# Output product of a gated state-space block: four fp32 matmuls a tile, or twelve float32r matmuls of rounded halves

## The chip, the cores and the metric

One Trainium2 chip, one core. The metric is the device time of one execution, in microseconds: the median over several runs. TensorE (PE in the profile) multiplies, VectorE (DVE), ScalarE (ACT) and GpSimd (POOL) work on tiles, SyncE (SP) issues the DMAs.

## The reference

`x` is 8 x 2048 x 256 in fp32. The block is a simplified state-space layer, then a feed-forward layer on weights and inputs rounded to a 4-bit grid in blocks of 16, each followed by a residual sum and a layer norm:

```python
xz = x @ W_in; x_proj, z = split(xz)            # 256 -> 2 * 512
x_conv = silu(causal_conv4(x_proj) + conv_b)
ssm = x_conv @ W_xproj                          # 512 -> 33: delta, B, C
delta = softplus(ssm[..., 0])
h_mean = einsum('bld,bln->bdn', x_conv, delta * B) / L
y = einsum('bdn,bln->bld', h_mean, C) + D * x_conv
y = y * silu(z)
x = layernorm(x + y @ W_out)                    # 512 -> 256, the product of this change
gate, up = fp4(x) @ fp4(w_gate).T, fp4(x) @ fp4(w_up).T
h = silu(gate) * up                             # 704
x = layernorm(x + fp4(h) @ fp4(w_down).T)
```

## The kernel before

The sequence axis is cut into 32 groups (`NSUP`) of 512 positions, four groups a batch element. A step of the kernel is a *unit*: group index `g_` and j = 0 to 3. Each engine has one queue, written out by hand; `walk(body)` runs the same loop over units on each of them, and semaphores couple them. Within a unit the engines work at different things: u = 4 g_ + j is the channel block whose input projection is made; v = u - 1 the block in the convolution; w = u - 20 the block (five groups behind, `LAG`) whose output y is formed and gated; and `to, tx, tg, td, tz` = w - 4 to w - 8 are tiles of 128 positions in the output product and first layer norm, in the rounding of x, in gate and up, in the down product and in the output. Up to `g_ == LAG` there is only input work and weight preparation (the opening), from `g_ > NSUP` on no input work (the end part).

Before the change the gated block is one fp32 buffer `g`, 128 x 2 x 4 x 512, two groups deep. VectorE's `skip` (L1128) writes D * x_conv + y from bank `pc` into it, GpSimd (L460) multiplies it in place by silu(z) and signals `g_ready`; in the end part VectorE does it in one step (`gated`, L1245) after TensorE's `skip_product` (L593). One unit later `output_projection` (L608) multiplies a tile of all four channel blocks with `wout`, in fp32:

```python
for c in range(NB):
    mm = pe.matmul(bank[:, 0:DM], g[:, (second(s) + 1) % 2, c, j * P:(j + 1) * P],
                   wout[:, c, :], start=(c == 0), stop=(c == NB - 1))
```

The other large products are made of float32r halves already, three products for one (`split_product`, L532). TensorE's order in a steady unit: gate and up (bank pgu), input projection (pa), transposes of h (L572), y product (L583), output product (L608), [j = 2: partial state L619], state projection (L635, which writes bank pc and waits for `skip`), transposes (L648, L658), z projection (pb), [j = 3: L678], down product (pd, L532 with wd).

What follows an output product: VectorE sums with the residual (L1218), ScalarE squares (L802), GpSimd makes the norm's factors (L411, L413, L415, on 128x1), ScalarE applies them (L904, `r1_rows`), and in the next unit VectorE rounds the tile to codes (L1001, L1005, L1009, L1013, L1019, L1022, the same lines as for h: 704 wide for h, 256 for x). On GpSimd the order in a steady unit is: norm of `tz`, x products (L427), history (L446), gate (L460), `conv_sum` (L450), norm of `to` (L411 to L415), h products (L470, L472). On ScalarE, in j = 0 units, softplus with two table loads (L808 to L983) comes right behind L904; in the next unit follow the squares (L802), the magnitude of x (L867) and the silu of the gate (L872), for which VectorE's L1190 waits.

Of the kernel before, what the change touches and what calls it, by code (L numbers as in the profile page):

```python
# [52 lines left out]
def block_kernel(nc, x, x_t, W_in, conv_w, conv_b, W_xproj, D_skip, W_out, w_gate, w_up, w_down, out):  # L53
# [26 lines left out]
    with ExitStack() as ctx:  # L80
# [13 lines left out]
        wout = sb("wout", [P, NB, DM])  # L94
# [30 lines left out]
        g = sb("g", [P, 2, NB, ST])  # L125
# [76 lines left out]
        yd_done = sem("yd_done")  # L202
        g_ready = sem("g_ready")
        xres_landed = [sem("xres_landed0"), sem("xres_landed1")]
# [37 lines left out]
        scratch = sb("scratch", [P, 5 * GW + 2 * FF + KM * P])  # L242
        flat_g = g[:, :, :, :].rearrange("p a b c -> p (a b c)")
        raw_g = scratch[:, 0:GW]
        raw_u = flat_g[:, GW + 9 * (GW // QB):2 * GW + 9 * (GW // QB)]
        raw_d = scratch[:, 5 * GW:5 * GW + 2 * FF]
        twice_d = scratch[:, 5 * GW + 2 * FF:5 * GW + 2 * FF + KM * P]
        quant_w = [scratch[:, n * GW:(n + 1) * GW] for n in range(1, 4)]
        w_big = [scratch[:, 4 * GW:5 * GW], flat_g[:, 0:GW], raw_g]

        at = [0]

        def over_scratch(width):

            at[0] += width
            assert at[0] <= scratch.shape[1]
            return scratch[:, at[0] - width:at[0]]

# [8 lines left out]
        GQ = GW // QB  # L267
        w_small = [[flat_g[:, GW + (3 * n + r) * GQ:GW + (3 * n + r + 1) * GQ] for r in range(3)]
                   for n in range(3)]
# [57 lines left out]
        def _(q):  # L327
# [19 lines left out]
            def body(g_, s, b):  # L347
                i = g_ - LAG
                for j in range(TPS):
# [6 lines left out]
                    if exists(w + 1):  # L356

                        n, half = (j + 1) % 2, 16 * (2 * i + (j + 1) // 2 + 1)
                        wait_apart(q, (xc_saved[n], half), (sz_saved[n], half), (g_ready, w))
                        q.dma_start(xl[:, n, :], xc_hbm[w + 1]).then_inc(xl_landed[n], 16)  # L360
                        q.dma_start(zl[:, n, :], sz_hbm[w + 1]).then_inc(zl_landed[n], 16)
# [22 lines left out]
        def _(pool):  # L384
# [33 lines left out]
            def body(g_, s, b):  # L418
                i = g_ - LAG
                for j in range(TPS):  # L420
# [35 lines left out]
                    if p2 and g_ <= NSUP:  # L456

                        pool.wait_ge(yd_done, w + 1)
                        pool.wait_ge(zl_landed[j % 2], 16 * (2 * i + j // 2 + 1))
                        pool.tensor_tensor(g[:, second(s) % 2, j, :], g[:, second(s) % 2, j, :], zl[:, j % 2, :],  # L460
                                           ALU.mult).then_inc(g_ready, 1)
                    if p1 and g_ > LAG:
                        conv_sum()
                    if exists(to) and g_ <= NSUP:
                        layer_norm(to, ssq1_done, r1_ready, rs1_eps, rs1_done, nm1_done, sum1, ssq1, rs1, nm1)
                    if exists(tg):
# [6 lines left out]
                                           spread(qsh[:, :, 1]), ALU.mult).then_inc(hprod_done, 1)  # L473
                    if j == 0 and exists(v):
# [38 lines left out]
        def _(pe):  # L513
# [62 lines left out]
            def y_product(j, s, b, g_, v, w):  # L576

                wait_apart(pe, (h_ready, b - 1 if s == 0 else b), (ct_ready, g_ - LAG + 1), (g_ready if g_ > NSUP else yd_done, w),
# [16 lines left out]
            def output_projection(j, s, i, g_, to, tz):  # L595
# [8 lines left out]
                if i == 1 and j == 0:  # L604
                    pe.wait_ge(w_landed, 32)
# [93 lines left out]
            def body(g_, s, b):  # L699
                i = g_ - LAG  # L700
                tail = exists(g_ - 1, NSUP)
                for j in range(TPS):
# [19 lines left out]
                    if g_ > NSUP:  # L722
# [48 lines left out]
        def _(act):  # L771
# [10 lines left out]
            def weight_magnitudes(u):  # L782

                if u in BIG_AT:
                    n = BIG_AT.index(u)
                    act.wait_ge(wq_link, CODED[n])
                    act.activation(w_big[n][:, 0:W_WIDTH[n]], quant_w[n][:, 0:W_WIDTH[n]], ACT.Abs, scale=TWO22)\
# [29 lines left out]
            def body(g_, s, b):  # L817
                i = g_ - LAG
                tail = exists(g_ - 1, NSUP)
                for j in range(TPS):  # L820
# [47 lines left out]

                    def gate_silu():
# [37 lines left out]
                    if g_ > NSUP:  # L907
# [16 lines left out]
                        if exists(tz):  # L924
                            out_rows()
                        continue
                    if g_ <= LAG:
# [5 lines left out]
                        weight_copies(u)  # L933
                        if exists(v):
                            conv_copy()
                        if j == 2:
# [23 lines left out]
                    if exists(tz):  # L960
                        out_rows()
                    if p1 and td < 0:
# [35 lines left out]
        def _(dve):  # L998
# [87 lines left out]
            def body(g_, s, b):  # L1086
                i = g_ - LAG
                tail = exists(g_ - 1, NSUP)
                for j in range(TPS):
# [32 lines left out]
                    def skip():  # L1122
                        dve.wait_ge(y_pe, w + 1)
                        dve.wait_ge(xl_landed[j % 2], 16 * (2 * i + j // 2 + 1))
                        at_least(dve, o_pe, 4 * i - 4)
                        if w == 0:
                            dve.wait_ge(w_landed, 32)
                        dve.scalar_tensor_tensor(g[:, second(s) % 2, j, :], xl[:, j % 2, :], dsk[:, j:j + 1], pc[:, :],  # L1128
# [110 lines left out]
                    def gated():  # L1239
                        if w == 4 * (NSUP - LAG + 1):  # L1240
                            dve.wait_ge(g_ready, w)
                        dve.wait_ge(y_pe, w + 1)
                        dve.wait_ge(zl_landed[j % 2], 16 * (2 * i + j // 2 + 1))
                        at_least(dve, o_pe, 4 * i - 4)
                        dve.tensor_tensor(g[:, second(s) % 2, j, :], pc[:, :], zl[:, j % 2, :],  # L1245
                                          ALU.mult).then_inc(g_ready, 1)
# [26 lines left out]
                    if g_ <= LAG:  # L1273
# [9 lines left out]
                        weight_codes(u)  # L1283
                        if j == 1 and 2 <= g_ < LAG:
# [80 lines left out]
```

## Time and profile before

| | us |
|---|---|
| median of 3 runs | 1985.98 (1985.72 to 1989.41) |
| the profiled execution, its own time | 1988.75 |
| its span, first to last instruction | 1987.0 |
| TensorE busy | 1920.3 (97%) |
| VectorE busy | 1578.8 (79%) |
| ScalarE busy | 1265.9 (64%) |
| GpSimd busy | 1102.5 (55%) |
| mean granted TensorE clock | 0.986 of 2.4 GHz |

Busy shares are means over an opening, a steady part and an end part. An engine's busy time counts its instructions from issue to end, waits for a memory port included. A record of a matmul is listed with its modelled end, so the distance between starts tells more than its duration.

### The profile page before, as it was taken

How to read it: one execution, taken by the hardware profiler on the slowest of the kernel's cores; microseconds unless marked ns; L12 is line 12 of the kernel's file. 1: busy time of each engine (PE TensorE's matmuls, PEld its weight loads, DVE VectorE, ACT ScalarE, POOL GpSimd, SP SyncE). 2: the span in 40 equal slices, each digit the busy share in tenths (PEclk: the TensorE clock that was granted, in tenths of full speed). 3: DMA queues.
4: the chain of work that ended last, by engine and by line, in shares of the span. 5: the costliest groups of instructions: out<-in, count | busy, mean ns of one | idle time of the engine just before them, and what ended most of it. 6: DMA issues, size and time to landing. Idle time of an engine off the chain costs nothing. (4 is left out here: it accounts for less than half of the span.)

```text
span 1987.0 us, 34279 instructions
## 1 busy us (share of the span) xinstructions
PE 1920.3 (97%) x10180; PEld 1540.1 (78%) x10180; DVE 1578.8 (79%) x3549; ACT 1265.9 (64%) x2617; POOL 1102.5 (55%) x1758
## 2 busy tenths in 40 slices
PE   6898999999999999999999999999999999999996
PEld 5665788888878888888788788888888888777775
DVE  5645788878888888888888888888788887788885
ACT  6776666666666666666666666666666666544443
POOL 3434555556555656655556665565565556555553
PEclk8898999999999999999999999999999999999998
DMA  5234233232322322323223232232323223222210
GB/s 167 96 122 144 91 100 103 89 109 99 102 100 98 99 95 99 109 94 109 96 85 107 99 109 96 99 104 88 109 99 101 100 88 99 69 65 73 72 38 16
DMA packets 120309, 190.60 MB, mean 96 GB/s; under 512 B 15040, under 2 KB 49728, under 8 KB 120128
## 3 DMA queue, kind: packets, MB, share of 16 engines
q1 hardware_dynamic: 120128, 188.42, 28.5%
q8 instruction: 85, 1.39, 0.3%
q14 instruction: 96, 0.79, 0.1%
HBM read 104.48 MB, written 83.89 MB: 95 GB/s over the span
## 5 line engine op out<-in xcount | busy, mean ns | idle before, releaser
L532 PE MATMUL pgu<-wgu_hi,xqT 128*128 128x512 f32 (+1 forms) x1536 | 427.1, 386 | 7.6 <-issue 6.5
L532 PEld LDWEIGHTS pgu<-wgu_hi,xqT 128*128 128x128 f32 x1536 | 278.7, 189 | 72.0 <-issue 9.9
L532 PE MATMUL pd<-wd_hi,hqT 128*128 128x256 f32 (+1 forms) x1536 | 315.9, 297 | 5.2 <-issue 2.1
L532 PEld LDWEIGHTS pd<-wd_hi,hqT 128*128 128x128 f32 (+1 forms) x1536 | 247.7, 190 | 26.6 <-issue 4.8
L1019 DVE SCALAR_TENSOR_TENSOR scratch<-scratch 128x256 f32<-128x256 f32 (+2 forms) x258 | 171.8, 666 | 96.7 <-ACT scratch L898 77.4
L411 POOL TENSOR_SCALAR rs<-ssq 128x1 f32<-128x1 f32 x256 | 72.4, 283 | 310.3 <-issue 297.3
L532 PE MATMUL pgu<-wgu_lo,xqT 128*128 128x512 f32 (+1 forms) x768 | 228.0, 378 | 0.0
L1104 DVE SCALAR_TENSOR_TENSOR acc<-xps,cw,acc 128x512 f32<-128x512 f32 x256 | 200.3, 782 | 30.8 <-POOL acc L450 26.2
L608 PE MATMUL pd<-wout,g 128*128 128x256 f32 x864 | 215.4, 392 | 0.0
L802 ACT ACTIVATE scratch<-scratch,sum 128x256 f32<-128x256 f32 x256 | 130.2, 509 | 123.4 <-DVE scratch L1164 118.4
L472 POOL TENSOR_TENSOR scratch<-hnq,qsh 128x704 f32<-128x704 bf16 x128 | 188.7, 1474 | 0.0
L608 PEld LDWEIGHTS pd<-wout,g 128*128 128x128 f32 x864 | 155.2, 189 | 42.6 <-issue 25.8
L413 POOL TENSOR_TENSOR rs<-rs,nhalf 128x1 f32<-128x1 f32 x256 | 170.4, 666 | 21.6
L532 PE MATMUL pd<-wd_lo,hqT 128*128 128x256 f32 x640 | 181.6, 284 | 0.0
L872 ACT ACTIVATE scratch<-pgu 128x704 f32<-128x704 f32 x128 | 96.6, 755 | 116.5 <-PE pgu L532 116.5
L450 POOL TENSOR_TENSOR acc<-acc,tap 128x512 f32<-128x512 f32 x128 | 164.3, 1284 | 11.4 <-ACT tap L846 11.4
L635 PEld LDWEIGHTS pc<-wxp,xcs 128*128 128x128 f32 x1024 | 134.6, 194 | 38.5 <-ACT xcs L829 21.6
L460 POOL TENSOR_TENSOR g<-g,early 128x512 f32<-128x512 f32 x112 | 143.1, 1278 | 35.5 <-DVE g L1128 35.2
L532 PEld LDWEIGHTS pgu<-wgu_lo,xqT 128*128 128x128 f32 x768 | 143.2, 189 | 23.5
L415 POOL TENSOR_SCALAR nm<-sum,rs 128x1 f32<-128x1 f32 x256 | 131.4, 513 | 43.8 <-POOL rs L413 43.8
L635 PE MATMUL pc<-wxp,xcs 128*128 128x33 f32 x1024 | 128.7, 271 | 24.6 <-ACT xcs L829 17.5
L427 POOL TENSOR_TENSOR scratch<-xnq,qsx 128x256 f32<-128x256 bf16 x128 | 81.3, 635 | 118.6 <-DVE xnq L1022 115.5
(140 smaller groups left out, 4489.8 us busy)
## 6 DMA issues: line engine op xcount, KB each, us to landing
sz_hbm<-szs SPq DMA_DIRECT2D x128, 256.0 KB, 2.0
xc_hbm<-xcs SPq DMA_DIRECT2D x128, 256.0 KB, 2.0
early<-xc_hbm SPq DMA_DIRECT2D x128, 256.0 KB, 2.7
early<-sz_hbm SPq DMA_DIRECT2D x128, 256.0 KB, 3.0
xin<-in_x_t_dram SPq DMA_DIRECT2D x32, 512.0 KB, 4.7
xres<-in_L_attn_x_dram SPq DMA_DIRECT2D x128, 128.0 KB, 2.4
out_dram<-scratch SPq DMA_DIRECT2D x128, 128.0 KB, 1.7
early<-in_L_attn_W_in_dram SPq DMA_DIRECT2D x2, 512.0 KB, 4.7
```

Of the source, the lines that this page charges most:

```text
L413: pool.tensor_tensor(rs[:, :], rs[:, :], nhalf[:, :], ALU.pow).then_inc(rs_done, 1)
L415: pool.tensor_scalar(nm[:, :], total[:, :], rs[:, :], -1.0 / DM, ALU.mult, ALU.mult)\
L450: pool.tensor_tensor(acc[:, j % 2, :], acc[:, j % 2, :], tap0[:, j % 2, :], ALU.add).then_inc(tap_done, 1)
L460: pool.tensor_tensor(g[:, second(s) % 2, j, :], g[:, second(s) % 2, j, :], zl[:, j % 2, :], ALU.mult).then_inc(g_ready, 1)
L472: pool.tensor_tensor(blocks(hq[:, 0:FF]), blocks(hnq[:, :]), spread(qsh[:, :, 1]), ALU.mult).then_inc(hprod_done, 1)
L532: mm = pe.matmul(bank, lhsT, rhs, start=(m == 0), stop=(m == len(pairs) - 1))
L608: mm = pe.matmul(bank[:, 0:DM], g[:, (second(s) + 1) % 2, c, j * P:(j + 1) * P], wout[:, c, :], start=(c == 0), stop=(c == NB - 1))
L635: mm = pe.matmul(pc[:, t * NX:(t + 1) * NX], xcs[:, jb % 2, t * P:(t + 1) * P], wxp[:, jb, :], start=True, stop=True)
L802: act.activation(dev[:, 0 if ssq is ssq1 else 1, :], r, ACT.Square, bias=total[:, :], scale=-1.0 * DM, accum_out=ssq[:, :]).then_inc(ssq_d ...
L872: act.activation(hbuf[:, 0:FF], pgu[:, 0:FF], ACT.Silu).then_inc(sg_ready, 1)
L1019: return dve.scalar_tensor_tensor(v, big, HALF_STEP, v, ALU.max, ALU.add)
L1104: dve.scalar_tensor_tensor(acc[:, jb % 2, :], xps[:, jb % 2, k:k + ST], cw[:, jb, k:k + 1], acc[:, jb % 2, :], ALU.mult, ALU.add).then_inc ...
```

## The change

The gated block is kept as two float32r halves, `g_hi` (rounded) and `g_lo` (the rest), and so is W_out (`wo_hi`, `wo_lo`). The output product of a tile is hi x hi, hi x lo and lo x hi: twelve float32r matmuls in place of four fp32 ones. Both halves are kept for one group only: blocks and tiles swap places in the buffer from group to group, so that a block may be written once the tile that lay there is multiplied. `skip` and the gate now work in a small buffer `gx` (two blocks); ScalarE copies it to `g_hi` (`gate_high`), GpSimd subtracts (`gate_rest`) and signals `g_ready`. The signal after the gate alone is `gate_done`. In ScalarE's queue `gate_high` stands, in the opening, behind `conv_copy` and ahead of `split_input`, `c_copy` and softplus; in the steady part behind `out_rows` (L887); in the end part last in the unit. W_out is split once in the opening (units 17 and 18). The weights are quantised in place, with buffers rearranged. In the end part `skip_product` goes ahead of the output product. The core of the diff:

```diff
-        g = sb("g", [P, 2, NB, ST])
+        g_hi = sb("g_hi", [P, NB, TPS, P], F32R)
+        g_lo = sb("g_lo", [P, NB, TPS, P], F32R)
...
+        def gated_block(half, i, c):
+            return half[:, c, :, :] if i % 2 == 0 else half[:, :, c, :]
+
+        def gated_tile(half, i, c, t):
+            return half[:, c, t, :] if i % 2 == 0 else half[:, t, c, :]
...
@@ gpsimd
-                        pool.tensor_tensor(g[:, second(s) % 2, j, :], g[:, second(s) % 2, j, :], zl[:, j % 2, :],
-                                           ALU.mult).then_inc(g_ready, 1)
+                        pool.tensor_tensor(gx[:, j % 2, :], gx[:, j % 2, :], zl[:, j % 2, :],
+                                           ALU.mult).then_inc(gate_done, 1)
+
+                    def gate_rest():
+                        pool.wait_ge(g_high, w + 1)
+                        pool.tensor_tensor(gated_block(g_lo, i, j), tiles_of(gx[:, j % 2, :]),
+                                           gated_block(g_hi, i, j), ALU.subtract).then_inc(g_ready, 1)
                     if p1 and g_ > LAG:
                         conv_sum()
+                    if p2 and g_ <= NSUP:
+                        gate_rest()
...
                         pool.tensor_tensor(blocks(hq[:, 0:FF]), blocks(hnq[:, :]),
                                            spread(qsh[:, :, 1]), ALU.mult).then_inc(hprod_done, 1)
+                    if p2 and g_ > NSUP:
+                        gate_rest()
...
@@ tensor, output_projection
+                pairs = []
                 for c in range(NB):
-                    mm = pe.matmul(bank[:, 0:DM], g[:, (second(s) + 1) % 2, c, j * P:(j + 1) * P],
-                                   wout[:, c, :], start=(c == 0), stop=(c == NB - 1))
-                mm.then_inc(o_pe, 1)
+                    high, low = gated_tile(g_hi, i - 1, c, j), gated_tile(g_lo, i - 1, c, j)
+                    pairs += [(high, wo_hi[:, c, :]), (high, wo_lo[:, c, :]), (low, wo_hi[:, c, :])]
+                split_product(bank[:, 0:DM], DM, pairs).then_inc(o_pe, 1)
...
@@ tensor, end part
+                        if p2:
+                            skip_product(j, i, w)
                         if exists(to):
                             output_projection(j, s, i, g_, to, tz)
-                        if p2:
-                            skip_product(j, i, w)
...
@@ scalar
+                    def gate_high():
+                        act.wait_ge(gate_done, w + 1)
+                        at_least(act, o_pe, 4 * (i - 1) + j + 1)
+                        act.activation(gated_block(g_hi, i, j), tiles_of(gx[:, j % 2, :]), ACT.Copy).then_inc(g_high, 1)
...
+                        if u == 17:
+                            act.wait_ge(w_landed, 32)
+                            act.activation(wo_hi[:, :, :], wout, ACT.Copy).then_inc(wo_h, 1)
...
@@ vector
-                        at_least(dve, o_pe, 4 * i - 4)
+                        at_least(dve, g_ready, w - 1)
...
+                        if u == 18:
+                            dve.wait_ge(wo_h, 1)
+                            dve.tensor_tensor(wo_lo[:, :, :], wout, wo_hi[:, :, :], ALU.subtract).then_inc(wo_l, 1)
```

## Rows read from the trace of the kernel before

**Rows 1.** Busy time by stretch: steady part, end part. Columns as in the head row.

```profile
400.00:600.00 200.00, 200.00 (x1085) 162.94 (x1085) 164.66 (x379) 134.48 (x281) 119.64 (x191) 1.00 0.31 103
1750.00:1850.00 100.00, 97.54 (x509) 77.97 (x508) 88.98 (x220) 49.69 (x115) 52.33 (x83) 1.00 0.26 80
```

**Rows 2.** Groups of instructions by line: busy, mean ns | idle before, releasers.

```profile
L780 ACT ACTIVATE xt_hi<-xin 128x512 fp32r<-128x512 f32 x64 | 36.6, 623 | 0.2 <-DMA xin<-in_x_t_dram 0.2
```

**Rows 3.** Timeline, steady part: start, us, engine, instruction, [idle before <-releaser].

```profile
1052.33 1.28 POOL L450 TENSOR_TENSOR acc<-acc,tap 128x512 f32<-128x512 f32 x1
...
1053.53 0.89 DVE L1013 SCALAR_TENSOR_TENSOR scratch<-scratch,qsh 128x704 f32<-128x704 f32 x1
...
1054.88 0.28 PE L532 MATMUL pd<-wd_hi,hqT 128*128 128x256 f32 x1
...
1054.98 0.19 POOL L411 TENSOR_SCALAR rs<-ssq 128x1 f32<-128x1 f32 x1 [1.37 <-issue]
...
1055.26 0.55 POOL L413 TENSOR_TENSOR rs<-rs,nhalf 128x1 f32<-128x1 f32 x1
...
1055.54 0.89 DVE L1019 SCALAR_TENSOR_TENSOR scratch<-scratch 128x704 f32<-128x704 f32 x1 [0.59 <-ACT scratch L898]
...
1056.54 0.89 DVE L1022 SCALAR_TENSOR_TENSOR hnq<-scratch 128x704 bf16<-128x704 f32 x1
1056.56 0.71 PE L532 MATMUL pd<-wd_hi,hqT 128*128 128x256 f32 x3
1056.60 0.60 ACT L904 ACTIVATE scratch<-scratch,nm,rs 128x256 f32<-128x256 f32 x1 [0.60 <-POOL nm L415]
...
1059.39 1.53 DVE L1104 SCALAR_TENSOR_TENSOR acc<-xps,cw,acc 128x512 f32<-128x512 f32 x2
...
1062.34 0.88 DVE L1190 TENSOR_TENSOR scratch<-scratch,pgu 128x704 f32<-128x704 f32 x1
...
1063.74 1.99 PE L608 MATMUL pd<-wout,g 128*128 128x256 f32 x8
1063.85 0.75 DVE L1128 SCALAR_TENSOR_TENSOR g<-early,dsk,pc 128x512 f32<-128x512 f32 x1 [0.62 <-PE pc L583]
...
1065.57 0.64 PE L635 MATMUL pc<-wxp,xcs 128*128 128x33 f32 x5
...
1079.24 1.06 PE L619 MATMUL pc<-xct,dB 128*48 128x512 f32 x2
```

**Rows 4.** Timeline of the end part, VectorE and GpSimd.

```profile
1788.85 0.89 DVE L1013 SCALAR_TENSOR_TENSOR scratch<-scratch,qsh 128x704 f32<-128x704 f32 x1
...
1789.01 0.79 POOL L411 TENSOR_SCALAR rs<-ssq 128x1 f32<-128x1 f32 x1 [0.79 <-issue]
...
1790.60 0.97 POOL L415 TENSOR_SCALAR nm<-sum,rs 128x1 f32<-128x1 f32 x1 [0.17 <-POOL rs L413]
1790.60 0.92 DVE L1019 SCALAR_TENSOR_TENSOR scratch<-scratch 128x704 f32<-128x704 f32 x1 [0.52 <-ACT scratch L898]
...
1792.43 0.68 DVE L1245 TENSOR_TENSOR g<-pc,early 128x512 f32<-128x512 f32 x1
...
1792.85 1.43 POOL L472 TENSOR_TENSOR scratch<-hnq,qsh 128x704 f32<-128x704 bf16 x1
...
1794.48 0.42 DVE L1013 SCALAR_TENSOR_TENSOR scratch<-scratch,qsx 128x256 f32<-128x256 f32 x1
...
1795.10 0.89 DVE L1190 TENSOR_TENSOR scratch<-scratch,pgu 128x704 f32<-128x704 f32 x1 [0.20 <-ACT scratch L872]
...
1799.48 0.89 DVE L1013 SCALAR_TENSOR_TENSOR scratch<-scratch,qsh 128x704 f32<-128x704 f32 x1
```

**Rows 5.** Timeline of the opening, first gated block.

```profile
149.38 1.28 ACT L808 ACT_TABLE_LOAD   x1
149.50 1.29 POOL L460 TENSOR_TENSOR g<-g,early 128x512 f32<-128x512 f32 x1
...
149.57 2.58 DVE L1104 SCALAR_TENSOR_TENSOR acc<-xps,cw,acc 128x512 f32<-128x512 f32 x2 [1.90 <-POOL acc L450]
```

More of the change, by code:

```diff
@@ L202, in block_kernel @@
         yd_done = sem("yd_done")
+        gate_done = sem("gate_done")
+        g_high = sem("g_high")
         g_ready = sem("g_ready")
+        wo_h = sem("wo_h")
+        wo_l = sem("wo_l")
         xres_landed = [sem("xres_landed0"), sem("xres_landed1")]
@@ L241, in block_kernel, with from_scratch @@
         zl = early[:, 2 * ST:4 * ST].rearrange("p (n c) -> p n c", n=2)
[L242 to L249, printed above, removed]
+        scratch = sb("scratch", [P, 4 * GW + 9 * (GW // QB) + 2 * FF + KM * P + NB * DM])
         at = [0]
-        def over_scratch(width):
+        def from_scratch(width):
             at[0] += width
@@ L257, in over_scratch, with tiles_of @@
             return scratch[:, at[0] - width:at[0]]
+        raw_g, raw_u, raw_d = from_scratch(GW), from_scratch(GW), from_scratch(2 * FF)
+        quant_w = [raw_g, raw_u, raw_d]
+        twice_d = from_scratch(KM * P)
+        BIG = at[0]
+        w_big = [from_scratch(GW), from_scratch(GW)]
+        w_big.append(w_big[0])
+        GQ = GW // QB
+        w_small = [[from_scratch(GQ) for r in range(3)] for n in range(3)]
+        wout = from_scratch(NB * DM).rearrange("p (c d) -> p c d", c=NB)
+        def tiles_of(ap):
+            return ap.rearrange("p (t n) -> p t n", t=TPS)
+        def gated_block(half, i, c):
+            return half[:, c, :, :] if i % 2 == 0 else half[:, :, c, :]
+        def gated_tile(half, i, c, t):
+            return half[:, c, t, :] if i % 2 == 0 else half[:, t, c, :]
+        later = [0]
+        def over_scratch(width):
+            later[0] += width
+            assert later[0] <= scratch.shape[1]
+            return scratch[:, later[0] - width:later[0]]
         hbuf = over_scratch(2 * FF)
@@ L266, in block_kernel @@
         outb = over_scratch(2 * DM).rearrange("p (t d) -> p t d", t=2)
[L267 to L269 removed]
+        gx = over_scratch(2 * ST).rearrange("p (n c) -> p n c", n=2)
         raw_w, W_WIDTH = (raw_g, raw_u, raw_d), (GW, GW, 2 * FF)
@@ L358, in body @@
                         n, half = (j + 1) % 2, 16 * (2 * i + (j + 1) // 2 + 1)
-                        wait_apart(q, (xc_saved[n], half), (sz_saved[n], half), (g_ready, w))
+                        wait_apart(q, (xc_saved[n], half), (sz_saved[n], half), (gate_done, w))
                         q.dma_start(xl[:, n, :], xc_hbm[w + 1]).then_inc(xl_landed[n], 16)
@@ L576, in y_product @@
             def y_product(j, s, b, g_, v, w):
-                wait_apart(pe, (h_ready, b - 1 if s == 0 else b), (ct_ready, g_ - LAG + 1), (g_ready if g_ > NSUP else yd_done, w),
+                wait_apart(pe, (h_ready, b - 1 if s == 0 else b), (ct_ready, g_ - LAG + 1), (gate_done if g_ > NSUP else yd_done, w),
                            (ssm_added, capped(v, NT)))
@@ L925, in body @@
                             out_rows()
+                        if exists(w) and g_ <= NSUP + LAG - 1:
+                            gate_high()
                         continue
@@ L961, in body @@
                         out_rows()
+                    if exists(w):
+                        gate_high()
                     if p1 and td < 0:
```

19 lines of the change are left out of this document (12 added, 7 removed).

## The prediction

> **What bounds the kernel now.** I read the stretches of time first, then one full round of the periodic part in order of time, then the waits inside it. In the middle of the run TensorE is busy all 200 of 200 us at clock 1.00, VectorE 164.66, ScalarE 134.48, GpSimd 119.64 [rows 1]. There every microsecond taken from TensorE's queue is worth one, as long as nobody else is late. After about 1740 us the picture is another: VectorE 88.98 of 100 and TensorE 97.54 [rows 1], units repeating every 10.63 us (L1013 at 1788.85 and 1799.48 [rows 4]), in a loop through VectorE that does not contain the output product: TensorE's gate/up product, ScalarE's silu, VectorE from L1190 to L1228, TensorE again.
>
> **The output product.** The four matmuls of a tile are eight records (x8), so an fp32 matmul of 256 columns is two. They start at 1063.74 and the next product, L635, at 1065.57 [rows 3]: 1.83 us a tile, 0.229 a record. The new product is twelve float32r matmuls of 256 columns. The down product is made of just these: from the start of its first at 1054.88 to the one at 1056.56 lie 14 of them [rows 3], 0.120 each. Twelve take 1.44. Saved: 0.39 us a tile. What stands ahead of it in the queue, the y product of 48 rows, is the same in either kernel, so I leave that gap as it is.
>
> The Trainium skill (TensorE: Matmul & The Clock Gate, Back-to-back issue gap) gives N/2.4 + 2.5 ns for a warm matmul: 109 ns for 256 columns and twice 107 plus 2.5 for an fp32 record, which would save 0.42 a tile. The rows are 0.120 and 0.229, and the rows decide.
>
> Were TensorE alone in the world, the 108 tiles of the groups up to `g_ == NSUP` (27 groups, `g_` 6 to 32) would give 42 us. The other 20 lie beside the loop above: their sum stands behind VectorE's work on the h block, so they give nothing.
>
> **What is added.** Per tile a ScalarE copy of 128x512 to float32r, 0.62 us by its nearest row [rows 2], and a GpSimd subtraction of 128x512 with two SBUF inputs, 1.28 us by the row of the same shape, L450 [rows 3]. By busy time both fit: a unit is some 14 us (L635 to L619 is 13.67), so 200 us hold 14, and GpSimd goes from 119.64 to about 138, ScalarE from 134.48 to 143. In the steady part the copy stands behind `out_rows`, where ScalarE idles for the transposes; nothing behind it is late. The subtraction stands behind `conv_sum` (L450), directly in front of the layer norm L411, L413, L415. It is this one that I follow, because GpSimd and VectorE hold each other up whenever both read two SBUF operands. Three places show it. L411 on one column took 0.79 when it started at 1789.01, inside VectorE's L1013 (1788.85 to 1789.74), and ended 0.06 after it [rows 4]; free, it takes 0.19 [rows 3]. L415, started together with L1019 at 1790.60, took 0.97. The other way round, two L1104 took 2.58 and not 1.53 [rows 3] when they started at 149.57, 0.07 after GpSimd's L460 had begun [rows 5]: 1.05 lost where 1.22 of L460 was left. So who is late loses what is left of the other, less 0.13 to 0.17. The Trainium skill (SBUF — State Buffer, Who interferes with whom) says that a VectorE instruction with two SBUF inputs contends with a GpSimd one that reads SBUF and that the first to issue keeps the port for its whole length. The trace agrees, with the three numbers above.
>
> *Steady part, hand-over from a j=0 to a j=1 unit [rows 3].* L1013 is issued at 1053.53, L450 ends at 1053.61, and GpSimd, with the next instruction waiting in its queue, issues it a little before that end, by my estimate at 1053.56. VectorE is 0.03 ahead, so I let it win. The subtraction waits to 1054.42 and ends 1.15 later, 1055.57. L1019, issued at 1055.54, goes next, to 1056.46. L411, before at 1054.98, now ends at 1056.52. L1022 follows L1019 by 0.11 and again is just ahead of L413, which ends at 1057.88 (0.42 behind L1022); L415 follows by 0.17 and takes some 0.25, an estimate from L411, the same kind, with 0.19. ScalarE's L904 waits for it: about 1058.35 and not 1056.60, 1.75 late. In a j=1 unit softplus with its two table loads stands right behind L904, so all of ScalarE is 1.75 late, its silu L872 too, and with it VectorE's L1190, which waits for that: 1064.09 and not 1062.34. It takes 0.88, L1128 another 0.75 less an overlap of 0.04: it ends at 1065.68. The state product L635 shares bank pc and waits for L1128: it starts at 1065.73. Before it was 1065.57, and TensorE alone, with two output products shortened (j=0 and j=1), would be there at 1064.79. The wait eats 0.94: this leg is 0.16 slower than before instead of 0.78 faster. From L635 to the partial state L619 at 1079.24 nothing binds anew (VectorE gets there 0.1 to 0.2 before TensorE), so it gains its 0.39: -0.23 so far. In the j=2 unit 3.6 us of L619 let everybody catch up, L411 isn't due until after the subtraction, and the leg to the next j=0 gains 0.39 again. Sum: -0.62 a group of four units where -1.56 was on offer. 108 tiles are 27 groups; 25 of them have this form: -15.5. The first, in which the feed-forward work only begins, gives 4 x 0.39 = -1.6. The last, with TensorE waiting already, 0.
>
> *End part, 16 units with a gate [rows 4].* There L472 ends at 1794.28 and the subtraction is next in line; the gated block was ready at 1793.11 (L1245) and its copy by 1793.8. It starts at 1794.23, 0.25 before L1013 of the x codes (1794.48), and runs to 1795.51. VectorE loses 1.03 - 0.17 = 0.86, of which L1190's wait for ScalarE (it starts 1795.10, could at 1794.82) hides 0.28. L1190 is in the loop: +0.58 a unit, 16 units: +9.3.
>
> *Opening.* At the first gated block ScalarE would go on to softplus at 149.38; `gate_high` now stands in front and waits for L460, which ends at 150.79 [rows 5], and takes 0.62: +2.05. Two later blocks of that group hold the input split and the C copy for about 0.5 each: +1.0. Splitting W_out (128x1024) costs ScalarE about 1.2 (twice L780) and VectorE about 1.3 (L1013's 0.89 for 704 elements, scaled), once, in gaps like the 1.90 that VectorE idled before L1104 [rows 5]; uncovered it would be 2.5. The new load order, the quantisation in place and the waits on `gate_done` at the point where `g_ready` was cost nothing: the same event, at the same place in the DMA queue. In the end part the skip product moves ahead of the output product; a matmul of 128x512 in fp32 is two records, so the output sum finds its operand some 0.9 us later, less the 0.39 saved. I take that as hidden behind VectorE's earlier work; bare, it would be 0.5 x 16 = 8 us, inside the range.
>
> Sum: -15.5 - 1.6 + 9.3 + 3.0 = -4.8 on the profiled execution's 1988.75 (span 1987.0 and 1.75 around it), 1983.95. The median of the runs is 1985.98; the same difference gives **1981.2 us**.
>
> **Rivals.**
> A. The forecast: steady gain mostly eaten in the j=0 to j=1 leg, end part slower. 0.42. Its own range: 1974 to 1989, for the leg's wait may be 0.3 more or less and the opening 1 to 5 us.
> B. At L450's end the subtraction gets the port and not L1013 (they are 0.03 apart). Then VectorE is 1.15 later in every unit but GpSimd's layer norm only 0.5 late; in the j=1 unit L1128 is back in time, and a wait of some 0.25 at L619 is left: -1.3 a group, -33 - 1.6 + 12.3 = -22, 1964. For it: L460 beat L1104 with 0.07 of a lead. Against: L1019 won a tie. 0.22.
> C. The subtraction meets nobody, as L460 and L450 meet only PSUM readers today: -42 + 3 = -39, 1947. The overlaps in rows 3 and 4 speak against it. 0.08.
> D. Slower: the same late layer norm also holds TensorE at the state product in j=0 and j=3 units. There L1128 ends 0.97 before L635 is due, 0.58 once the product is shorter; if VectorE comes more than 0.97 late relative to now in one more unit of each group, the steady gain is gone. From -0.62 it goes to 0 and a little above: 0 to +4, +12.3, so about +14, 2000. For it: three of the four hand-overs have the same order of GpSimd. Against: only j=1 has softplus behind L904. 0.28.
>
> The product by the page's gap instead of the row would only move A by about 1 us and changes no chance.
>
> **How the numbers follow.** A difference of 0.2% is 4 us, about what can be told from none. A lies at -4.8, half of it beyond: faster 0.22, same 0.15, slower 0.05. B and C are faster, 0.30. D is slower 0.25, same 0.03. Together faster 0.52, same 0.18, slower 0.30. The range leaves out C and the far half of D and of the low side of B: 1959 to 2000.
>
> **What would show it.** After: L608 gone, a product of twelve records about 1.44 long before L635; L411 behind L1019 in j=0, 1 and 3 units and L904 later by 1.7; TensorE idle for about 0.9 at L635 in one unit in four; groups of four units 0.6 shorter; in the end part 11.2 and not 10.63 between units, with the x codes' L1013 taking 1.3. A group shorter by 1.3 makes B right, by 1.5 C, one as long as now D. If the end part stays at 10.6, the port is not held by the subtraction, and the forecast is wrong by its largest positive term.

## The result, and the profile of the changed kernel

The changed kernel takes 1997.56 us (median of five runs, 1996.58 to 1998.87), the kernel before 1986.58 beside it on the same chip. The ratio is 1.0051, 95% interval 1.0037 to 1.0066: slower by half a per cent. The forecast was 1981.2, faster by 0.24%. The range held the time, the sign was wrong. The profiled execution took 1996.68 us (span 1994.6), 7.9 more than the profiled one of before (1988.75). The medians lie 11.0 apart: of the five runs of the kernel before, three lie at 1985.7 to 1986.6 and two at 1989.4 to 1989.8, and its profiled execution is near the upper ones.

Busy time by stretch, changed kernel, against [rows 1]. Behind the stretch and its length stand the busy times of TensorE's matmuls, its weight loads, VectorE, ScalarE and GpSimd (with the number of instructions), the granted clock of TensorE, the busy share of the DMA engines and GB/s:

```profile
400.00:600.00 200.00, 198.43 (x1146) 162.99 (x1144) 165.06 (x376) 141.56 (x295) 147.82 (x206) 1.00 0.30 102
1750.00:1850.00 100.00, 91.87 (x518) 73.30 (x518) 91.20 (x204) 52.69 (x116) 60.43 (x91) 1.00 0.23 71
```

In the steady part TensorE now idles 1.57 of 200 us. GpSimd is 28 us busier and not the 18 that fourteen subtractions of 1.28 make. In the end part TensorE has lost 5.7 of 100. The groups say where GpSimd's time is:

```profile
L490 POOL TENSOR_TENSOR g_lo<-scratch,g_hi 128x512 fp32r<-128x512 f32 x128 | 236.3, 1846 | 7.0 <-ACT g_hi L910 7.0
L947 ACT ACTIVATE scratch<-scratch,nm,rs 128x256 f32<-128x256 f32 x128 | 76.8, 600 | 203.8 <-POOL nm L440 203.8
L671 PE MATMUL pc<-wxp,xcs 128*128 128x33 f32 x1024 | 132.1, 274 | 39.6 <-ACT xcs L867 19.5 <-issue 16.8 <-DVE hacc L1186 3.1
```

L490 is the new subtraction: 1.85 us each, though it takes 1.27 when it meets nobody. L947 is the old L904, L440 the old L415: ScalarE waits 203.8 us for the layer norm.

To place the 7.6 us of span, I take the start of the gate/up product of every tile from the timelines; tiles 0 and 4 close the opening and the first group, 4 to 100 are 24 steady groups, 100 to 106 the seam, 106 to 124 the end part with its 16 gated units.

| Stretch | before | changed | difference | forecast |
|---|---|---|---|---|
| start to tile 0 | 190.80 | 196.21 | +5.4 | +3.0 |
| tiles 0 to 4 | 61.73 | 60.61 | -1.1 | -1.6 |
| tiles 4 to 100 | 1402.72 | 1396.58 | -6.1 | -14.9 |
| tiles 100 to 106 | 81.65 | 81.85 | +0.2 | -0.6 |
| tiles 106 to 124 | 191.52 | 201.29 | +9.8 | +9.3 |
| tile 124 to the end | 58.58 | 58.06 | -0.5 | 0 |

The two stretches ahead of tile 4 vary from run to run: with the end part's edit below, the same kernel up to there, tile 0 starts at 195.63 and tiles 0 to 4 take 61.82, so the -1.1 says little.

A steady group was 17.29 + 14.00 + 13.58 + 13.58 us (units j = 2, 3, 0, 1) and is 16.97 + 13.70 + 13.27 + 14.25. Three units are 0.3 shorter, the fourth 0.67 longer. This fourth unit, in order of time (answers to [rows 3]):

```profile
1053.87 0.89 DVE L1065 SCALAR_TENSOR_TENSOR scratch<-scratch,qsh 128x704 f32<-128x704 f32 x1
1053.91 2.00 POOL L490 TENSOR_TENSOR g_lo<-scratch,g_hi 128x512 fp32r<-128x512 f32 x1
1055.61 1.05 DVE L1071 SCALAR_TENSOR_TENSOR scratch<-scratch 128x704 f32<-128x704 f32 x1 [0.32 <-ACT scratch L941]
1056.00 0.71 POOL L436 TENSOR_SCALAR rs<-ssq 128x1 f32<-128x1 f32 x1
1056.77 0.89 DVE L1074 SCALAR_TENSOR_TENSOR hnq<-scratch 128x704 bf16<-128x704 f32 x1
1056.79 1.27 POOL L438 TENSOR_TENSOR rs<-rs,nhalf 128x1 f32<-128x1 f32 x1
1058.23 0.27 POOL L440 TENSOR_SCALAR nm<-sum,rs 128x1 f32<-128x1 f32 x1 [0.17 <-POOL rs L438]
1058.54 0.60 ACT L947 ACTIVATE scratch<-scratch,nm,rs 128x256 f32<-128x256 f32 x1 [2.47 <-POOL nm L440]
1059.16 1.28 ACT L846 ACT_TABLE_LOAD   x1
...
1063.35 0.74 ACT L915 ACTIVATE scratch<-pgu 128x704 f32<-128x704 f32 x1
...
1064.28 0.88 DVE L1242 TENSOR_TENSOR scratch<-scratch,pgu 128x704 f32<-128x704 f32 x1
...
1065.08 0.74 DVE L1180 SCALAR_TENSOR_TENSOR scratch<-early,dsk,pc 128x512 f32<-128x512 f32 x1
1065.15 0.28 PE L567 MATMUL pd<-wo_hi,g_lo 128*128 128x256 f32 x1
1065.92 0.27 PE L671 MATMUL pc<-wxp,xcs 128*128 128x33 f32 x1 [0.49 <-issue]
...
1066.53 0.68 DVE L1251 TENSOR_TENSOR hqT<-pe_,hqT 128x512 fp32r<-128x512 f32 x1
...
1067.13 0.41 DVE L1254 TENSOR_TENSOR hqT<-pb,hqT 128x256 fp32r<-128x256 f32 x1
...
1067.36 0.41 PE L694 MATMUL pe_<-ident,scratch 128*128 128x128 f32 x2
...
1067.69 0.70 PE L567 MATMUL pb<-xt_hi,win_hi 128*128 128x512 f32 x2
```

L1065, L1071, L1074 are the old L1013, L1019, L1022. The subtraction starts 0.04 behind VectorE's division and waits for it (2.00 and not 1.28); the one-column L436 waits for L1071, L438 for L1074. L947 comes 1.32 us behind the gate/up product of its unit (1057.22) where L904 came 0.60 ahead of it. Softplus, the silu L915, L1242 and L1180 follow, and the state product L671 waits for L1180. TensorE's last output matmul starts at 1065.15, the next product at 1065.92 and not 0.12 later: 0.65 of waiting. The profile names no releaser for it ("issue"); the kernel's wait is for L1180, which ends 0.10 before.

Two more waits follow in the same unit. The transposes of x (L694, the old L658) wait for L1251, which ends at 1067.21, the z product for L1254, which ends at 1067.54; each starts 0.15 behind. In the kernel before, the same three starts lie 0.81, 0.47 and 0.14 apart from L635 on (L648, L658, pb), here 0.89, 0.55 and 0.33, in every steady group: another 0.33 in all.

### The profile page after: what moved, and what is told of

The parts are those of the page before. It is cut to its first block and busy times, and to the rows that moved or that the text cites. A ratio compares the mean times of both kernels' runs of the same rounds, so it can differ in the third digit from the quotient of the medians.

```text
span 1994.6 us, 35686 instructions
## 1 busy us (share of the span) xinstructions
PE 1899.6 (95%) x10692; PEld 1536.4 (77%) x10692; DVE 1603.1 (80%) x3550; ACT 1335.0 (67%) x2746; POOL 1348.3 (68%) x1886
## 5 line engine op out<-in xcount | busy, mean ns | idle before, releaser
L1071 DVE SCALAR_TENSOR_TENSOR scratch<-scratch 128x704 f32<-128x704 f32 (+2 forms) x259 | 184.9, 714 | 91.0 <-ACT scratch L941 57.8
L490 POOL TENSOR_TENSOR g_lo<-scratch,g_hi 128x512 fp32r<-128x512 f32 x128 | 236.3, 1846 | 7.0 <-ACT g_hi L910 7.0
L438 POOL TENSOR_TENSOR rs<-rs,nhalf 128x1 f32<-128x1 f32 x256 | 213.8, 835 | 21.3
L436 POOL TENSOR_SCALAR rs<-ssq 128x1 f32<-128x1 f32 x256 | 102.2, 399 | 185.6 <-issue 166.5
L947 ACT ACTIVATE scratch<-scratch,nm,rs 128x256 f32<-128x256 f32 x128 | 76.8, 600 | 203.8 <-POOL nm L440 203.8
L505 POOL TENSOR_TENSOR scratch<-hnq,qsh 128x704 f32<-128x704 bf16 x128 | 182.9, 1429 | 0.0
L475 POOL TENSOR_TENSOR acc<-acc,tap 128x512 f32<-128x512 f32 x128 | 165.2, 1291 | 11.4 <-ACT tap L884 11.4
L671 PEld LDWEIGHTS pc<-wxp,xcs 128*128 128x128 f32 x1024 | 130.1, 196 | 54.0 <-issue 28.0
L671 PE MATMUL pc<-wxp,xcs 128*128 128x33 f32 x1024 | 132.1, 274 | 39.6 <-ACT xcs L867 19.5
L485 POOL TENSOR_TENSOR scratch<-scratch,early 128x512 f32<-128x512 f32 x112 | 143.9, 1285 | 23.5 <-DVE scratch L1180 23.3
L567 PE MATMUL pd<-wo_hi,g_hi 128*128 128x256 f32 x432 | 131.6, 305 | 0.0
L471 POOL COPY hist<-xps 128x3 f32<-128x3 f32 x128 | 27.2, 213 | 153.1 <-ACT acc L878 153.1
```

What stands on the lines that cost most here:

```text
L436: pool.tensor_scalar(rs[:, :], ssq[:, :], 1.0 / DM ** 3, EPS, ALU.mult, ALU.add).then_inc(eps_done, 1)
L438: pool.tensor_tensor(rs[:, :], rs[:, :], nhalf[:, :], ALU.pow).then_inc(rs_done, 1)
L475: pool.tensor_tensor(acc[:, j % 2, :], acc[:, j % 2, :], tap0[:, j % 2, :], ALU.add).then_inc(tap_done, 1)
L485: pool.tensor_tensor(gx[:, j % 2, :], gx[:, j % 2, :], zl[:, j % 2, :], ALU.mult).then_inc(gate_done, 1)
L490: pool.tensor_tensor(gated_block(g_lo, i, j), tiles_of(gx[:, j % 2, :]), gated_block(g_hi, i, j), ALU.subtract).then_inc(g_ready, 1)
L505: pool.tensor_tensor(blocks(hq[:, 0:FF]), blocks(hnq[:, :]), spread(qsh[:, :, 1]), ALU.mult).then_inc(hprod_done, 1)
```

## The experiments

The edits below are made in the changed kernel. [rows 3] and [rows 4] have the same places of before; line numbers of each fence are those of its own kernel. The diffs are shortened. Group and unit lengths are from the starts of the gate/up products.

**No low half.** No subtraction; ScalarE's copy makes the block ready, and the passes that read the low half read the high half.

```diff
-pool.tensor_tensor(gated_block(g_lo, i, j), tiles_of(gx[:, j % 2, :]),
-                   gated_block(g_hi, i, j), ALU.subtract).then_inc(g_ready, 1)
-act.activation(gated_block(g_hi, i, j), ...).then_inc(g_high, 1)
+act.activation(gated_block(g_hi, i, j), ...).then_inc(g_ready, 1)
-high, low = gated_tile(g_hi, i - 1, c, j), gated_tile(g_lo, i - 1, c, j)
+high, low = gated_tile(g_hi, i - 1, c, j), gated_tile(g_hi, i - 1, c, j)
```

> The low half of the gated block is left out: no subtraction on GpSimd, ScalarE's copy alone makes a block ready, and the third kind of pass reads the high half in its place, so the product keeps its twelve passes. All else is the changed kernel. Theory (the subtraction's place on GpSimd makes the layer norm's small operations late in the steady part and holds the x codes' division in the end part): the unit after j = 0's step falls from 14.25 to 13.27 us, the group of four units from 58.19 to 57.2, the end part's unit from 11.23 to 10.6; 25 groups x 1.0 and 16 units x 0.6 are 35 us, so about 1962 us. Rival (the copies on ScalarE or the product's own 1.52 us eat the gain): groups stay at 58.2, end units at 11.2, and the time at 1995 or so.

1960.84 us, ratio to the kernel before 0.9864 (0.9851 to 0.9878). Group 57.22, its fourth unit 13.27, the end part's unit 10.64, first gate/up product at 193.46. The 37 us between this and the changed kernel are what the subtraction costs; the copies on ScalarE stayed, and cost nothing outside the opening: all four steady units are 0.3 shorter than in the kernel before, the end part's unit is as it was.

**A memset in its place.**

```diff
-g_lo = sb("g_lo", [P, NB, TPS, P], F32R)
+g_lo = sb("g_lo", [P, NB, TPS, P])
...
-pool.tensor_tensor(gated_block(g_lo, i, j), ..., ALU.subtract).then_inc(g_ready, 1)
+at_least(pool, g_ready, w)
+pool.memset(g_lo[:, 0:3, :, :], 0.0).then_inc(g_ready, 1)
...
-high, low = gated_tile(g_hi, i - 1, c, j), gated_tile(g_lo, i - 1, c, j)
+high, low = gated_tile(g_hi, i - 1, c, j), gated_tile(g_hi, i - 1, c, j)
```

> The subtraction is replaced by a memset of 1536 columns on GpSimd at the same place behind the same wait (about 1.3 us, writes SBUF and reads nothing); the third kind of pass reads the high half. It leaves out the low half of the gated block. Theory (GpSimd's reads of two SBUF operands and VectorE's hold each other up): the memset takes its 1.3 us always, the x codes' division in the end part is back at 0.43 us, the end part's unit at 10.6, and the steady group near 57.3, since the layer norm's small operations start only 0.3 us late; about 1965 us. Rival (it is the time that GpSimd's queue is taken, not what the operation reads): the steady group stays near 58.2 and the time near 1985 or more.

1964.16 us, 0.9883 (0.9869 to 0.9896). Group 57.34, end unit 10.64. The same hand-over, then the end part, of the memset's timeline:

```profile
1043.12 0.88 DVE L1065 SCALAR_TENSOR_TENSOR scratch<-scratch,qsh 128x704 f32<-128x704 f32 x1
1043.13 1.38 POOL L491 MEMSET g_lo<- 128x1536 f32 x1
1044.61 0.19 POOL L436 TENSOR_SCALAR rs<-ssq 128x1 f32<-128x1 f32 x1
1044.86 0.89 DVE L1071 SCALAR_TENSOR_TENSOR scratch<-scratch 128x704 f32<-128x704 f32 x1 [0.32 <-ACT scratch L941]
1044.88 1.28 POOL L438 TENSOR_TENSOR rs<-rs,nhalf 128x1 f32<-128x1 f32 x1
...
1836.55 1.38 POOL L491 MEMSET g_lo<- 128x1536 f32 x1
1836.82 0.42 DVE L1065 SCALAR_TENSOR_TENSOR scratch<-scratch,qsx 128x256 f32<-128x256 f32 x1
```

GpSimd's queue is taken for longer than by a free subtraction (1.38, all 128 of them between 1.37 and 1.41), beside the same VectorE work, and nobody is held: the division keeps its 0.42. Occupancy of the queue is thus not the cost. It leaves 0.12 a group: it made L436 later, so L438 lost its turn to L1071 by 0.02 and took 1.28. Of the three waits of the fourth unit the last alone is left, at the z product (0.28 behind L694 and not 0.14).

**A copy in its place.**

```diff
-pool.tensor_tensor(gated_block(g_lo, i, j), ..., ALU.subtract).then_inc(g_ready, 1)
+pool.tensor_copy(gated_block(g_lo, i, j), tiles_of(gx[:, j % 2, :])).then_inc(g_ready, 1)
```

> The subtraction is replaced by a GpSimd copy of the same block to the low half: one SBUF operand read and not two, same place, same wait (it leaves out the subtraction, so the low half holds the whole block). Its time alone is between 0.6 and 1.3 us, bounded from the 64-column casts (0.24 us) and the 512-column sums (1.28 us) of GpSimd. Theory (only an operation that reads two SBUF operands holds VectorE's and is held by them): as with the memset, division 0.43 us, end units 10.6, steady group at most 57.4, about 1963 us. Rival (any read by GpSimd does it): division above 0.8 us, end units above 10.8, steady group above 57.6.

1960.51 us, 0.9857 (0.9841 to 0.9874); group 57.22, end unit 10.64. The times are those of my theory, its reason is not:

```profile
1039.28 0.88 DVE L1064 SCALAR_TENSOR_TENSOR scratch<-scratch,qsh 128x704 f32<-128x704 f32 x1
1039.29 1.35 POOL L490 CAST g_lo<-scratch 128x512 fp32r<-128x512 f32 x1
...
1841.96 0.61 POOL L490 CAST g_lo<-scratch 128x512 fp32r<-128x512 f32 x1
1842.22 0.63 DVE L1064 SCALAR_TENSOR_TENSOR scratch<-scratch,qsx 128x256 f32<-128x256 f32 x1
```

Alone the copy takes 0.61. Behind L1064 it takes 1.35, and in the end part it holds L1064 for 0.21. One operand read from SBUF on GpSimd is enough to wait and to be waited for. The copy is cheap because it is short: held, it ends at 1040.64, about where a free subtraction would. So my "only two operands" is refuted for GpSimd's side, and the rival's mechanism holds without its price. The one-operand L411 of [rows 4], held to 0.79, had said so already.

**Layer norm ahead of the subtraction, steady part.**

```diff
-if p2 and g_ <= NSUP:
-    gate_rest()
 if exists(to) and g_ <= NSUP:
     layer_norm(to, ssq1_done, r1_ready, rs1_eps, rs1_done, nm1_done, sum1, ssq1, rs1, nm1)
+if p2 and g_ <= NSUP:
+    gate_rest()
```

> In the steady part alone GpSimd does the layer norm's three small operations ahead of the subtraction and not behind it; the same work. Theory: the scaling of the rows by ScalarE comes back from 1058.54 to about 1056.6, the unit of 14.25 us falls to 13.3, the group from 58.19 to 57.2, the end part stays at 11.23; 25 us less, about 1972 us, faster than the kernel before. Rival (the subtraction then runs against the codes' last step and makes the products of the codes late, so TensorE waits at the transposes instead): the group stays within 0.3 of 58.2 and the time within 5 of 1997.

1989.69 us, 1.0011 (1.0002 to 1.0020): a third of what was expected. The fourth unit was back at 13.27 as forecast, but the second went from 13.70 to 14.15, and in some groups the third too (24 groups: 57.91 on average). In the second unit, j = 3:

```profile
1080.47 1.29 POOL L490 TENSOR_TENSOR g_lo<-scratch,g_hi 128x512 fp32r<-128x512 f32 x1
1080.48 2.03 DVE L1074 SCALAR_TENSOR_TENSOR hnq<-scratch 128x704 bf16<-128x704 f32 x1
1082.59 0.30 POOL L503 TENSOR_TENSOR scratch<-hnq,qsh 128x64 f32<-128x64 bf16 x1 [0.83 <-DVE hnq L1074]
1082.84 1.87 POOL L505 TENSOR_TENSOR scratch<-hnq,qsh 128x704 f32<-128x704 bf16 x1
```

The subtraction now wins by 0.01 and holds L1074 (2.03 for 0.89); the products of the codes behind it on GpSimd end 2.0 us after the unit's gate/up product starts (1082.69) where they ended 0.4 after it. Theory and rival each had half.

**Only in step j = 0.**

```diff
+if p2 and g_ <= NSUP and j != 0:
+    gate_rest()
 if exists(to) and g_ <= NSUP:
     layer_norm(...)
+if p2 and g_ <= NSUP and j == 0:
+    gate_rest()
```

> As norm_first, but only in the step j = 0, whose softplus stands behind the layer norm's rows; in steps 1 to 3 the subtraction stays ahead of the layer norm. The same work. Theory (each place of the subtraction collides with what VectorE does there; only in j = 0 is the layer norm on the path): the unit that took 14.25 us takes 13.3, the one that the last experiment lengthened to 14.15 is back at 13.70, the group is 57.2 us: 24 us less than the changed kernel, about 1974. Rival (the collision is handed on from step to step whatever the order): a group of 57.7 or more, 1985 or more.

1972.20 us, 0.9917 (0.9903 to 0.9931). Group 57.22 (16.98, 13.71, 13.27, 13.27), the very length without a low half. The collision is still there, on an operation that can wait:

```profile
1043.04 0.65 POOL L440 TENSOR_SCALAR nm<-sum,rs 128x1 f32<-128x1 f32 x1 [0.17 <-POOL rs L438]
1043.65 1.27 POOL L490 TENSOR_TENSOR g_lo<-scratch,g_hi 128x512 fp32r<-128x512 f32 x1
1043.66 2.01 DVE L1076 SCALAR_TENSOR_TENSOR hnq<-scratch 128x704 bf16<-128x704 f32 x1
1043.72 0.60 ACT L949 ACTIVATE scratch<-scratch,nm,rs 128x256 f32<-128x256 f32 x1 [0.60 <-POOL nm L440]
```

**End part: the subtraction one unit later.** For j = 0 to 2, behind the product of the x codes.

```diff
 if exists(tx) and g_ > NSUP:
     x_values()
+if g_ > NSUP and p2 and j > 0:
+    gate_rest(w - 1, i, j - 1)
...
-if p2 and g_ > NSUP:
+if p2 and g_ > NSUP and j == 3:
     gate_rest()
```

> In the end part alone the subtraction of units j = 0 to 2 stands one unit later on GpSimd, behind the product of the x codes; that of j = 3 stays. Theory: the x codes' division takes 0.43 us and not 1.3 in 12 of 16 units, which fall from 11.23 to about 10.65 us: 7 us less, 1990 us. Rival (the subtraction holds the codes of the hidden block at its new place, or the copy on ScalarE is what makes the end part longer): units stay at 11.2.

1990.41 us, 1.0014 (1.0004 to 1.0023). Twelve units take 10.64, four 11.21; tiles 106 to 124 take 194.09 and not 201.29. The division beside the subtraction, changed kernel:

```profile
1840.12 1.27 POOL L490 TENSOR_TENSOR g_lo<-scratch,g_hi 128x512 fp32r<-128x512 f32 x1
1840.36 1.31 DVE L1065 SCALAR_TENSOR_TENSOR scratch<-scratch,qsx 128x256 f32<-128x256 f32 x1
1841.60 0.87 DVE L1242 TENSOR_TENSOR scratch<-scratch,pgu 128x704 f32<-128x704 f32 x1
```

and deferred:

```profile
1859.59 0.42 DVE L1067 SCALAR_TENSOR_TENSOR scratch<-scratch,qsx 128x256 f32<-128x256 f32 x1
1860.25 0.89 DVE L1244 TENSOR_TENSOR scratch<-scratch,pgu 128x704 f32<-128x704 f32 x1 [0.23 <-ACT scratch L917]
...
1862.61 1.30 POOL L457 TENSOR_TENSOR g_lo<-scratch,g_hi 128x512 fp32r<-128x512 f32 x1
...
1862.78 0.88 DVE L1055 TENSOR_REDUCE qsh<-scratch 128x44 f32<-128x704 f32 x1
```

At its new place it meets L1055, which has one SBUF input, and neither is longer.

**Both moves.**

> Both moves of the subtraction together: behind the layer norm in j = 0 of the steady part, one unit later in units 0 to 2 of the end part. The same work. Theory (the two costs lie in different stages and add up): 24 + 7 = 31 us less than the changed kernel, about 1966 us, ratio to the kernel before 0.99. Rival (one move gives back part of the other's gain, as at the seam between the stages): 1975 or more.

1964.40 us, 0.9875 (0.9861 to 0.9889). Tiles 4 to 100 take 1373.28, 106 to 124 take 194.11: the two costs add up. This is the best version that computes everything, 1.25% faster than the kernel before.

**And ScalarE's copy last in the opening.** On top of both moves, for `g_ <= LAG`:

```diff
 if exists(v):
     conv_copy()
-if exists(w):
-    gate_high()
 ...
     softplus(g_)
 ...
+if exists(w):
+    gate_high()
 weight_magnitudes(u)
```

> As j0_and_end, and in the opening ScalarE does its copy of the gated block behind the input's split, the C copy and the softplus, and not ahead of them. The same work. Theory (the copy ahead of the softplus and of the split of the next input makes the opening longer): the first gate product comes 1 to 3 us earlier than with j0_and_end, about 1964 us. Rival (in the opening it is the subtraction on GpSimd or the lower granted clock, not the copy's place): the first gate product within 0.7 us of that of j0_and_end, or later.

1966.03 us, 0.9885 (0.9871 to 0.9899), not apart from both moves. The first part went as expected: softplus loads its table at 149.53 and not 151.37, the fourth y product of the group starts at 170.18 and not 172.08. Then TensorE's granted clock falls where it did not before, and tile 0 comes at 199.59, later than with both moves alone (196.71). With both moves alone TensorE has 5.5 us at the lower clock between 156 and 162 us and none from 162 to 189, as in the changed kernel. This kernel:

```profile
156.00:162.00 6.00, 5.29 (x21) 3.59 (x20) 3.70 (x5) 3.85 (x8) 4.54 (x5) 0.81 0.40 129
162.00:170.00 8.00, 6.05 (x22) 2.58 (x21) 5.65 (x6) 6.17 (x11) 5.21 (x6) 1.00 0.53 184
170.00:180.00 10.00, 9.10 (x31) 6.50 (x31) 2.49 (x5) 3.73 (x8) 3.92 (x4) 0.60 0.54 169
180.00:189.00 9.00, 8.31 (x36) 7.09 (x36) 1.47 (x4) 3.62 (x7) 3.40 (x5) 0.69 0.24 75
```

and the changed kernel:

```profile
156.00:162.00 6.00, 6.00 (x20) 4.48 (x20) 4.54 (x5) 3.24 (x6) 4.01 (x5) 0.53 0.40 129
162.00:170.00 8.00, 7.77 (x32) 3.86 (x30) 5.33 (x7) 5.67 (x10) 4.77 (x5) 1.00 0.45 163
170.00:180.00 10.00, 6.71 (x38) 5.12 (x38) 5.14 (x8) 5.91 (x10) 4.90 (x7) 1.00 0.54 162
180.00:189.00 9.00, 8.31 (x50) 6.63 (x48) 2.86 (x10) 5.84 (x13) 5.70 (x11) 1.00 0.46 164
```

0.60 over 10 us and 0.69 over 9 us are 8.0 and 5.6 us at the lower of the two levels (1.2 GHz), where the changed kernel has none; from 156 to 162 us it has 5.6 and this one 2.3. That is some 10 us more at half speed. TensorE had idled 1.95 of the 8 us ahead of the fall, 0.23 in the changed kernel. That this is what made the clock fall is not shown: the changed kernel idles 3.29 of its next 10 us and keeps 1.00 in the 9 behind them. Nor is the clock shown to be all of the 2.9 us.

**No low half in the opening alone.**

```diff
-if p2 and g_ <= NSUP:
+if p2 and LAG < g_ <= NSUP:
     gate_rest()
...
```

(with the copy making these four blocks ready, and their tiles reading the high half twice)

> The low half is left out in the opening alone (four units; the four output tiles that read it take the high half twice): no subtraction there. All else is the changed kernel. Theory (the run without any low half had its first gate product 2.75 us earlier, and that was the subtraction in the opening): first gate product at 193.5 and not 196.2, the steady and the end part unchanged, 2.7 us less: about 1995. Rival (those 2.75 us are the lower granted clock falling on other work, not the subtraction's wait): the first gate product within 1 us of 196.2, with a different length at half clock.

1995.91 us, 1.0036 (1.0023 to 1.0049); the runs overlap with those of the changed kernel (1993.71 to 1997.26, 1996.58 to 1998.87). Tile 0 is at 193.96, 2.25 earlier (expected 2.7). But 0.65 of this was there before the first gated block, where the two kernels do the same: the first y product starts at 142.70 and not 143.35. From that start to tile 0 it is 51.26 us, where the changed kernel and the runs with the layer norm first, only in j = 0, the deferred end part and both moves have 52.86 to 53.05. So the opening's subtractions cost 1.6 to 1.8 us up to tile 0. By tile 4 the difference is lost in what two runs of the same kernel differ by: from the first y product it is 112.7 here, 113.5 in the changed kernel, 114.8 with the end part deferred.

**Sixteen passes.** The halves, copies and subtractions stay, the product is four f32 matmuls of the high halves; the low halves' part is left out.

```diff
-split_product(bank[:, 0:DM], DM, pairs).then_inc(o_pe, 1)
+for c in range(NB):
+    mm = pe.matmul(bank[:, 0:DM], gated_tile(g_hi, i - 1, c, j).bitcast(F32),
+                   wo_hi[:, c, :].bitcast(F32), start=(c == 0), stop=(c == NB - 1))
+mm.then_inc(o_pe, 1)
```

> The halves, their copies, waits and subtractions all stay as in the changed kernel, but the product is four f32 matmuls of the high halves (16 passes), as the kernel before did it. It leaves out the low halves' part of the product. Theory (the product saves 0.31 us a tile wherever TensorE is the bound): units of the steady part grow by 0.3 each but for the one of 14.25 us, in which TensorE waits 0.65 us and can hide it: group 59.1, 25 x 0.93 = 23 us, the end part's unit unchanged at 11.23 (it is not TensorE that bounds it): about 2021 us. Rival (the product isn't on the path, and the gain seen in the units comes from elsewhere): within 5 of 1997.

2017.02 us, 1.0144 (1.0130 to 1.0158). The group is 17.28 + 14.00 + 13.58 + 14.05, 58.92: three units are 0.31 longer, the fourth is 0.2 shorter than with twelve passes. The end part's unit stays at 11.23. So the passes are worth 0.31 us in three of four steady units; the fourth gives 0.2 of it back, since TensorE, being earlier, waits longer at the state product (0.65 us against 0.13); in the end part they are worth nothing. The expectation had the fourth unit unchanged, hence 59.1 and 2021.

## Why the prediction was wrong

**The product.** It saves 0.31 us a tile, not 0.39. Its twelve starts lie 0.118 apart but for the first step, 0.22, behind the y product of 48 rows; together 1.52 from the first to the next product's start, not 1.44. The fp32 product has the same in it: its first step is 0.32, the others 0.216,

```profile
1065.14 0.59 PE L608 MATMUL pd<-wout,g 128*128 128x256 f32 x2
```

the last two of the eight records, 0.43 us ahead of L635 at 1065.57. So the 0.229 of the prediction is no spacing but the product's length over eight, with the long first step in it, while I multiplied the bare spacing of the down product by twelve. The gap that I left "as it is" is the same 0.10 in either kernel, and I counted it in one alone. What makes it was not isolated.

**The fourth unit (hand-over from j = 0 to j = 1).** The links up to L671 were right: tie at L1065, L436 behind L1071, L438 behind L1074, ScalarE, L1242, L1180, L671. Against the start of the j = 0 unit L947 is 1.60 late, forecast 1.75 (the 1.92 above also has the 0.31 in it by which the j = 1 unit starts earlier). The wait at L671 is 0.65 us, forecast 0.94. What the forecast did not have are the two waits behind it, 0.33 together; with them the unit is 0.67 longer, forecast 0.55. The runs without a low half and with the layer norm first in j = 0, both with 13.27, have none of the three.

**The steady sum** is where the forecast failed most: -0.26 a group, not -0.62. In its own three legs, means of 24 groups:

| Leg | before | changed | difference | forecast | without a low half |
|---|---|---|---|---|---|
| gate/up of j = 0 to L635 (L671) in j = 1 | 21.94 | 21.97 | +0.02 | +0.16 | 21.32 |
| on to L619 (L655) in j = 2 | 13.67 | 13.68 | +0.01 | -0.39 | 13.36 |
| on to the gate/up of the next j = 0 | 22.83 | 22.54 | -0.29 | -0.39 | 22.54 |

The step that failed is the second: "From L635 to the partial state L619 nothing binds anew (VectorE gets there 0.1 to 0.2 before TensorE), so it gains its 0.39". VectorE does not get there first. In the kernel before, its L1199 ends 1.39 us behind the end of L1128, and TensorE's L658, which waits for it, starts 1.28 behind L635; once L635 starts right behind L1128, as the forecast had it, VectorE is the later of the two. The leg gains 0.31 by the product and loses 0.33 by the two waits. Against the forecast the second leg is 0.40 longer, the third 0.10, for the product's size, and the first 0.14 shorter (the wait at L671 is 0.29 less, its two products save 0.16 less): 0.36 a group. 24 groups make 8.7 of the 12.4 us that lie between the forecast's -4.8 and the +7.6 of span; 2.4 are the opening, the rest is the table's other rows. The forecast of the sign hung on a small margin, a gain of 1.17 less a loss of 0.55 a group: 0.2 us a group was enough to turn it.

**The end part** was right in size and cause: the division 1.31 (forecast 1.3), the unit 11.23 (11.2), +9.8 (+9.3). That the skip product ahead of the output product costs nothing there holds too: without the low half the unit is 10.64.

**The opening** was mis-sized, +5.4 and not +3.0. Softplus' 2.0 is in the trace (151.37 for 149.38) and the fourth y product is 4.3 later (172.08 for 167.78). What I had left out: the subtraction in front of the next input's split, which holds VectorE's L1089,

```profile
168.44 1.75 POOL L490 TENSOR_TENSOR g_lo<-scratch,g_hi 128x512 fp32r<-128x512 f32 x1 [0.74 <-ACT g_hi L910]
168.99 2.35 DVE L1089 TENSOR_TENSOR xt_lo<-xin,xt_hi 128x512 fp32r<-128x512 f32 x2
```

2.35 where the same pair took 1.29 in the kernel before; and the granted clock, 0.53 from 156 to 162 us where it was 0.82, though 0.74 from 189 to 196 us where it was 0.52. Without subtractions in the opening the pair is back at 1.30 and tile 0 comes 1.6 to 1.8 earlier, which is most of the 2.4 us. How much of this the spells at the lower clock carry, and what the rest is, stays open: each edit of the opening also moves these spells.

**The rivals.** B had the subtraction win the port behind L475 (the old L450); VectorE was 0.04 ahead there and won, as the forecast had it. C is refuted by the 2.00 of L490. D named the right sign, +14 on the span, and the wrong way: the first three units did not lengthen, they are 0.3 shorter.

**The port.** A GpSimd operation that reads SBUF and a VectorE one that reads two SBUF operands take turns; whoever issues later loses what is left of the other less 0.13 to 0.15: 2.00 - 1.28 with 0.85 left, 1.31 - 0.42 with 1.03 left, 2.01 - 0.89 with 1.26 left. The Trainium skill (SBUF — State Buffer, Who interferes with whom) says that a VectorE instruction with two SBUF inputs contends with a GpSimd instruction that reads SBUF, not with one that only writes it, and that issue order decides who blocks. The copy of 0.61 us that takes 1.35 agrees with it, and so does the memset, which reads nothing and kept its 1.37 to 1.41 in 128 cases.

## What to carry to other kernels

A new operation on a second engine is priced by what the other engine does in the same microseconds, not by its busy time: the same 1.28 us cost 37 us of 1997 at one set of places and 4 at another (1964.4 against 1960.8 without it). Where TensorE is the bound, moving work off it gains only in the units in which nobody else becomes late; look at each unit of the period by itself, and behind the first wait follow the late engine on: here it made TensorE wait twice more. A subtraction that collides everywhere is best put where its victim has slack, which may differ from step to step.

## What the runs showed of the hardware that was not expected

A one-column GpSimd operation of 0.55 us takes 1.27 when it is issued 0.02 behind a VectorE operation with two SBUF inputs (L438), so a collision costs the other's length however small one's own is. A product of 256 columns behind a matmul of 48 rows loses 0.10 us at its first step, in all 108 cases of either kernel: 0.22 and not 0.118 for float32r, 0.32 and not 0.216 for an fp32 record. GpSimd copies 128x512 from f32 to float32r in 0.61 us, half of what it takes to subtract it. And a change that makes the opening's dependencies shorter can make the opening longer, here by 2.9 us at tile 0, with some 10 us more at the lower clock.
